# Expert results finished in slot order: gathered residual and branch rows, and a scatter straight into the output

## What is computed

```python
x = x + s * g                                   # block 0
xn = _layernorm(x, axis=-1)
s = _L1_attn_ref(xn, ...)                       # Y + X: the branch rows
# expert layer
route = jax.nn.sigmoid(x @ router_w)            # x is xn here
max_ind = jnp.argmax(route, axis=1)
max_prob = jnp.take_along_axis(route, max_ind[:, None], axis=1)
for e in range(num_experts):
    h = jax.nn.silu(x @ gate_w[e]) * (x @ up_w[e])
    out = out + jnp.where((max_ind == e)[:, None], h @ down_w[e], 0.0)
out = out * max_prob
# end of block 1
x = x + s * _silu(out)
```

## Time and profile before

| | us |
|---|---|
| median of 3 runs | 370.25 |
| lowest and highest run | 370.02, 370.71 |
| span of the profiled execution | 370.6 |

### The profile page before, as it was taken

The page is one execution under the profiler, slowest core; times in us unless marked ns, Lnnn a source line. Parts: engine busy times, 40 slices in busy tenths (PEclk is TensorE's granted clock), DMA queues, the critical chain, the costliest instruction groups (busy, mean ns, idle before and its releaser), DMA issues.

```text
span 370.6 us, 4637 instructions
## 1 busy us (share of the span) xinstructions
PE 326.3 (88%) x1598; PEld 191.5 (52%) x1598; DVE 239.2 (65%) x473; ACT 154.4 (42%) x279; POOL 62.8 (17%) x64
## 2 busy tenths in 40 slices
PE   3849859999999999999999999989968999999730
PEld 3426636545555454455554555556554576666420
DVE  3999895977666677877958510499793644433305
ACT  1614722476766655553664555203113322332300
POOL 4372480000011000000000000014570111211211
PEclk9958997999999999999999999996998999999965
DMA  7960000000000000000000050093029960111015
GB/s 262 405 161 0 2 0 3 0 3 1 0 4 0 3 0 3 0 0 3 2 2 1 0 171 2 2 371 138 31 92 329 435 240 30 30 42 44 17 44 200
DMA packets 9914, 28.46 MB, mean 77 GB/s; under 512 B 1342, under 2 KB 6559, under 8 KB 8608
## 3 DMA queue, kind: packets, MB, share of 16 engines
q1 hardware_dynamic: 8976, 26.01, 19.3%
q0 software_dynamic: 912, 2.12, 1.5%
HBM read 24.86 MB, written 5.55 MB: 82 GB/s over the span
## 4 chain that ended last, share of the span: by engine, by line
PE 72%; DVE 17%; DMA 4%; issue 2%; POOL 2%; ACT 1%; DVEq 0%; SPq 0%; POOLq 0%
PE ps L1532 11%; PE ps L1477 8%; PE ps L1445 8%; PE ps L1545 7%; PE ps L1467 7%; PE ps L1586 6%; PE ps L1600 6%; PE ps L1608 5%; PE ps L1382 3%; DVE xn L1014 3%; PE ps L1407 2%; DVE nmax L1069 2%; POOL slot_rows L779 2%; PE ps L1361 2%; PE ps L1576 1%
## 5 line engine op out<-in xcount | busy, mean ns | idle before, releaser
L1069 DVE TENSOR_REDUCE nmax<-ps 128x1 f32<-128x512 f32 x128 | 85.8, 688 | 34.4 <-PE ps L1445 33.7
L880 ACT ACTIVATE shared<-ps 128x512 f32<-128x512 f32 x128 | 74.2, 594 | 53.9 <-PE ps L1467 52.8
L1445 PE MATMUL ps<-experts 96*128 96x512 bf16 x128 | 48.2, 384 | 1.8 <-DVE experts L1076 1.2
L1467 PE MATMUL ps<-experts 99*128 99x512 bf16 x128 | 48.5, 382 | 0.0
L1545 PE MATMUL ps<-shared,experts 128*128 128x256 f32 x128 | 38.0, 386 | 0.0
L1477 PE MATMUL ps<-shared,experts 128*32 128x512 f32 x256 | 34.1, 605 | 0.3 <-ACT shared L880 0.3
L1445 PEld LDWEIGHTS ps<-experts 96*128 96x128 bf16 x128 | 12.5, 98 | 36.8 <-DVE nmax L1069 18.2
L1545 PEld LDWEIGHTS ps<-shared,experts 128*128 128x128 f32 x128 | 23.3, 191 | 9.7 <-issue 3.4
L1382 PE MATMUL ps<-late_weights,xnT 128*128 128x512 f32 (+1 forms) x64 | 25.0, 542 | 0.7 <-DVE shared L1035 0.7
L769 POOL TENSOR_TENSOR experts<-experts,late_weights 128x768 f32<-128x768 f32 x1 | 1.8, 1809 | 130.9 <-ACT experts L870 130.9
L888 ACT ACTIVATE experts<-ps 96x1024 bf16<-96x1024 bf16 x18 | 18.0, 1020 | 12.5 <-PE ps L1407 12.4
(11 more groups left out here) (204 smaller groups left out, 536.3 us busy)
## 6 DMA issues: line engine op xcount, KB each, us to landing
experts<-in_experts SPq DMA_DIRECT2D x8, 1536.0 KB, 10.6
shared<-in_wgu SPq DMA_DIRECT2D x1, 2048.0 KB, 11.1
slot_rows<-in_empty SPq DMA_DIRECT2D x1, 1950.0 KB, 19.6
late_weights<-slot_rows SPq DMA_DIRECT2D x9, 130.0 KB, 2.3
x<-in_x SPq DMA_DIRECT2D x2, 512.0 KB, 5.7
shared<-in_wdn SPq DMA_DIRECT2D x1, 1024.0 KB, 13.1
shared<-expert_results SPq DMA_DIRECT2D x4, 256.0 KB, 3.7
out_x<-x SPq DMA_DIRECT2D x4, 256.0 KB, 2.0
```

Source lines behind the costliest of these rows:

```text
L880: nc.scalar.activation(probs[:, n % 2, hh, :], ps[:, 2 + hh % 2, :], ACT.Exp, scale=float(HD) ** -0.5).then_inc(s["exp_done"], 1)
L1069: nc.vector.tensor_reduce(nmax[:, 4 * t + hh:4 * t + hh + 1], ps[:, m % 2, :], AX, ALU.max, negate=True).then_inc(s["max_done"], 1)
L1445: nc.tensor.matmul(ps[:, m % 2, :], qs[0:KS, b, GR * g + hh, P * t:P * t + P], ks[0:KS, b, g, :], start=True, stop=True).then_inc(s["score ...
L1467: nc.tensor.matmul(ps[:, 2 + hh % 2, :], ks[0:KM, b, g, P * t:P * t + P], qs[0:KM, b, GR * g + hh, :], start=True, stop=True).then_inc(s[" ...
```

## The change

Rows are finished in the order of the slots. Both operands of the end, x and the branch rows, go into one DRAM table of token rows (`token_rows`, 1024 rows of 2 KB: x, then s). For each tile POOL gathers its 128 rows of this table by token number into one of four buffers (`gathered`, which lies in the memory of `x`), three tiles ahead. DVE multiplies the result with the gathered branch row and adds the gathered x row; POOL scatters the finished rows by token number straight into the output. Token numbers are changed from p + 128 j to 8 p + j, so that the output's layout [128, 8, 256] is a plain table of rows.

SP stores x after it has issued the third expert's load, and the branch rows after the last branch step, ahead of all reloads of row slots. As the branch rows come late, the results of tiles 0 to 6 are kept in `held`, and `final` finishes them later: 0 and 1 after result 4 in tile 5, 2 and 3 in tile 6, 4 and 5 in tile 7, and 6 ahead of result 7 in tile 8. From tile 7 on `result` does it all. A row slot is now loaded again only when the finished rows of its tile have landed in the output. The reload of the results, the four products and additions at the end and the four output stores are gone. The end waits for the scatters and for the gathers of up to three tiles that aren't there (their rows are all out of bounds).

```diff
-    put("token", p[:, None] + P * np.arange(NT)[None, :])
+    put("token", p[:, None] * NT + np.arange(NT)[None, :])
...
+    xg_dram = nc.dram_tensor("token_rows", (TOK, 2 * D), F32, kind="Internal").ap()
+    xg_rows = xg_dram.rearrange("(p j) d -> p j d", p=P)
+    out_rows = out.rearrange("p j d -> (p j) d")
...
+        held = Sa[:, 0:D * HELD].rearrange("p (j n) -> p j n", j=HELD)
+        gathered = x[:].rearrange("p (a c) n -> p a (c n)", a=GATHERED)
...
                 if e == FIRST_EXPERTS - 1:
+                    sp.wait_ge(s["x1_part"], B * TB // 2)
+                    sp.dma_start(xg_rows[:, :, 0:D], x[:]).then_inc(s["x_stored"], 16)
...
+            sp.wait_ge(s["branch_ready"], NT // 2)
+            sp.dma_start(xg_rows[:, :, D:2 * D], gx[:]).then_inc(s["g_stored"], 16)
+
             def reload_rows(i):
                 if i + XR < MT:
                     sp.wait_ge(s["xs_T"], i + 1)
-                    sp.wait_ge(y_store[i % 2], 16 * (i // 2 + 1))
+                    sp.wait_ge(out_store[i % GATHERED], 16 * (i // GATHERED + 1))
                     load_rows(i + XR)
...
             sp.wait_ge(s["results_stored"], 1)
-            for q in range(NT // 2):
-                sp.dma_start(yg[:, 2 * q:2 * q + 2, :], y_dram.rearrange("(j p) d -> p j d", p=P)[:, 2 * q:2 * q + 2, :]).then_inc(result_sem[q], 16)
-            for q in range(NT // 2):
-                sp.wait_ge(s["out_ready"], q + 1)
-                sp.dma_start(out[:, 2 * q:2 * q + 2, :], x[:, 2 * q:2 * q + 2, :]).then_inc(out_sem[q], 16)
-            for q in range(NT // 2):
-                sp.wait_ge(out_sem[q], 16)
...
+            def gather(i):
+                if i >= GATHERED:
+                    pool.wait_ge(out_store[i % GATHERED], 16 * (i // GATHERED))
+                pool.wait_ge(x_sem[i % XR], 16 * (i // XR + 1))
+                nc.gpsimd.indirect_dma_start(
+                    out=gathered[:, i % GATHERED, :], out_offset=None, in_=xg_dram[:, :], in_offset=by_token(i),
+                    bounds_check=TOK - 1, oob_is_err=False).then_inc(gather_sem[i % GATHERED], 16)
+
             def store(i):
-                pool.wait_ge(s["y_ready"], i + 1)
+                pool.wait_ge(s["out_ready"], i + 1)
                 nc.gpsimd.indirect_dma_start(
-                    out=y_dram[:, :], out_offset=bass.IndirectOffsetOnAxis(ap=slot_row(i, TOKEN_COL, TOKEN_COL + 1).bitcast(I32), axis=0),
-                    in_=ysb[:, i % 2, :], in_offset=None, bounds_check=TOK - 1, oob_is_err=False).then_inc(y_store[i % 2], 16)
+                    out=out_rows[:, :], out_offset=by_token(i),
+                    in_=gathered[:, i % GATHERED, 0:D], in_offset=None, bounds_check=TOK - 1, oob_is_err=False
+                ).then_inc(out_store[i % GATHERED], 16)
+                if i + GATHERED - 1 < MT:
+                    gather(i + GATHERED - 1)
 
             def all_stored(n):
-                for a in range(2):
-                    pool.wait_ge(y_store[a], 16 * ((n + 1 - a) // 2))
+                for i in range(n, min(n + GATHERED - 1, MT)):
+                    pool.wait_ge(gather_sem[i % GATHERED], 16 * (i // GATHERED + 1))
+                for a in range(GATHERED):
+                    pool.wait_ge(out_store[a], 16 * ((n + GATHERED - 1 - a) // GATHERED))
                 pool.sem_inc(s["results_stored"], 1)
 
+            pool.wait_ge(s["x_stored"], 16)
+            pool.wait_ge(s["g_stored"], 16)
+            for i in range(GATHERED - 1):
+                gather(i)
             for i in range(SURE):
                 store(i)
...
             def result(k):
                 dve.wait_ge(s["e_down"], k + 1)
-                if k >= 2:
-                    dve.wait_ge(y_store[k % 2], 16 * (k // 2))
                 nc.vector.tensor_scalar_mul(ysb[:, k % 2, :], ps[:, 6, 0:D], slot_row(k, PROB_COL, PROB_COL + 1)).then_inc(s["y_half"], 1)
...
+                if k < HELD:
+                    dve.wait_ge(s["y_tanh"], k + 1)
+                    nc.vector.scalar_tensor_tensor(held[:, k, :], ytanh, 1.0, ysb[:, k % 2, :], ALU.add, ALU.mult).then_inc(s["y_ready"], 1)
+                    return
+                row = gathered[:, k % GATHERED, :]
+                dve.wait_ge(s["y_half"], k + 1)
+                dve.wait_ge(gather_sem[k % GATHERED], 16 * (k // GATHERED + 1))
+                nc.vector.tensor_tensor(row[:, D:2 * D], ysb[:, k % 2, :], row[:, D:2 * D], ALU.mult).then_inc(s["product_ready"], 1)
+                dve.wait_ge(s["product_ready"], k + 1)
                 dve.wait_ge(s["y_tanh"], k + 1)
-                nc.vector.scalar_tensor_tensor(ysb[:, k % 2, :], ytanh, 1.0, ysb[:, k % 2, :], ALU.add, ALU.mult).then_inc(s["y_ready"], 1)
+                nc.vector.scalar_tensor_tensor(row[:, D:2 * D], ytanh, 1.0, row[:, D:2 * D], ALU.add, ALU.mult).then_inc(s["y_ready"], 1)
+                dve.wait_ge(s["y_ready"], k + 1)
+                nc.vector.tensor_tensor(row[:, 0:D], row[:, D:2 * D], row[:, 0:D], ALU.add).then_inc(s["out_ready"], 1)
+
+            def final(k):
+                row = gathered[:, k % GATHERED, :]
+                dve.wait_ge(s["y_ready"], k + 1)
+                dve.wait_ge(gather_sem[k % GATHERED], 16 * (k // GATHERED + 1))
+                nc.vector.tensor_tensor(row[:, D:2 * D], held[:, k, :], row[:, D:2 * D], ALU.mult).then_inc(s["product_ready"], 1)
+                dve.wait_ge(s["product_ready"], k + 1)
+                nc.vector.tensor_tensor(row[:, 0:D], row[:, D:2 * D], row[:, 0:D], ALU.add).then_inc(s["out_ready"], 1)
+
+            finals = {SURE - 3: (0, 1), SURE - 2: (2, 3), SURE - 1: (4, 5), SURE: (6,)}
```

More of the change, by code:

```diff
@@ L47 @@
 VW = 32
+HELD = SURE - 1
+GATHERED = 4
 QK_AT = 8192 + 2048 + NI * S
@@ L799, in _ @@
             tiles_from(pool, n_tiles, SURE, store, all_stored)
-            for q in range(NT // 2 - 1, NT // 2):
-                pool.wait_ge(result_sem[q], 16)
-                pool.wait_ge(s["branch_ready"], NT // 2)
-                nc.gpsimd.tensor_tensor(ya[:, 2 * q:2 * q + 2, :], yg[:, 2 * q:2 * q + 2, :], gx[:, 2 * q:2 * q + 2, :], ALU.mult
-                                        ).then_inc(s["product_ready"], 1)
         @block.scalar
@@ L1283, in tile, with last_rows @@
                 nc.vector.tensor_tensor(hm[:, i % 2, :], gated[:, i % 2, :], ps[:, 2 + i % 2, :], ALU.mult).then_inc(s["e_h"], 1)
+                last_rows(i)
+            def last_rows(i):
+                if i >= SURE:
+                    for k in finals.get(i, ()):
+                        final(k)
                 if i:
                     result(i - 1)
+                if i < SURE:
+                    for k in finals.get(i, ()):
+                        final(k)
             for i in range(SURE):
@@ L1297, in _ @@
             n_tiles = dve.value_load(tiles_n[0:1, 0:1], min_val=SURE, max_val=MT)
[L1298 to L1316 removed]
+            tiles_from(dve, n_tiles, SURE, tile, last_rows)
         @block.tensor
```

35 lines of the change are left out of this document (10 added, 25 removed).

## The result

The changed kernel takes 364.45 us (median of four runs, 363.6 to 365.07) beside 370.42 us for the kernel before on the same chip: a ratio of 0.984, with an interval of 0.9805 to 0.9873. Five of those ten runs lie over 1.5% above the fastest and count as slow; the median of the other five is 365.12. The forecast was 361.2, in a range of 359.7 to 364.8: the first median lies just inside that range, the second above it. The sign and the path of the tail up to its last wait were right; the gain is 3.5 to 6 us where the forecast had 9.

The account below looks back on a forecast made before the run. PE bounds the expert tiles, then a 14.3 us tail leaves it idle. Scatter at 357.60, empty gather from 358.87 to 361.05, plus 0.5 to the end gives 361.55; less 0.35, 361.2 us, range 359.7 to 364.8.

Parts of the forecast that it names:

- To the start of the last scatter: Tail: scaling at 354.94, STT end at 356.34, residual addition to 356.83, GpSimd's scatter 0.77 us later at 357.60.
- Scatter to empty gather: Tail on GpSimd: consecutive indirect DMAs start 1.27 us apart, so the gather for absent tile 13 starts at 358.87.
- Empty gather to the end of the waits: Tail: the out-of-bounds gather lands after 2.18 us, at 361.05; bounds 0.96 to 2.4 us.
- Rival 1: Tail: the empty gather lands at once and the last scatter decides the end, 360.0 us; chance 0.12.
- From there to the end: Block end: 0.5 us from last landing to span end, with GpSimd's drain taken as 0 (bounds 0 and 3.4).
- rival 2: Block end: GpSimd's drain or code behind its nested branches is exposed, up to 3.4 us, giving 364.6; chance 0.21.
- the 0.35: Span to time: the runs' median, 370.25, lies 0.35 us below the profiled span of 370.6; taken off 361.55.
- reload of slot 8: Expert tiles: SP's reload takes 2.1 us to 327.2, PE transposes at 329.21; 2.0 us of cover, the tightest joint.
- Rival 3: Expert tiles: slot 8's reload is late and PE stalls about 5 us, total 366 to 368; chance 0.09.
- Rival 4: GpSimd's queue: 2 KB-row gathers cost far more to issue and bound the kernel, 378 at 3.3 us each; chance 0.05.
- Gather 7: Expert tiles: GpSimd's backlog lands this gather at about 338, 0.5 us after VectorE asks, inside VectorE's cover.
- VectorE beside GpSimd: Expert tiles: indirect-DMA issue doesn't hold VectorE, arithmetic does; otherwise up to 1.9 us a tile in tiles 5 to 7.

Follow-up runs that it names:

- second series: The changed kernel with no edit, measured again beside the kernel before with the experiments: 366.9 us (ten runs, 361.58 to 368.75), ratio 0.990.

## Why the prediction was right, and where it was not

**The tail, step by step.** Counted from the start of the last scaling (predicted at 354.94, found at 352.09):

- To the start of the last scatter: predicted 357.60 - 354.94 = 2.66, measured 354.83 - 352.09 = 2.74. The product did run beside the tanh (352.61 to 353.03) and cost nothing. A dependent 256-column step came 0.46 us after the one before, not 0.485, and GpSimd's start 0.83 us after its releaser, not 0.77.
- Scatter to empty gather: predicted 1.27, measured 1.33.
- Empty gather to the end of the waits: predicted 2.18 (between 0.96 and 2.4), measured 358.4 - 356.16 = 2.24. A gather with all its rows out of bounds costs what a full one of the same kind costs in the quickest case (2.1 us, view of L797 below). Rival 1, an end at the scatter's landing, is thereby out.
- From there to the end: predicted 0.5, measured 3.2. **This is the step that failed.** "POOL's last instruction has ended 1.2 us before the landing it waits for, so there is nothing left to drain" took the drain for a wait for running work. The kernel with the products on VectorE, the one with 14 more gathers and the early drains show a cost for every indirect DMA since the last drain, 82 ns each, due whenever the drain comes. Its bounds, 0 and 3.4, did hold it, and rival 2 with its 0.21 is what happened, and not the forecast with its 0.50: 361.2 + 2.8 = 364.0, against 364.45 in the first series. That the first median falls into the range is owed to rival 2's share of it.

Sum: 2.74 + 1.33 + 2.24 + 3.2 = 9.51, against 2.66 + 1.27 + 2.18 + 0.5 = 6.61 predicted.

**From span to time.** "The median of the runs lies 0.35 below that span" compared two executions, as did the sentence ahead of the prediction that took the profiled execution's span for its time. The time of one and the same execution was 1.8 us above its span in the kernel before, and the profiled execution was 2.2 us above the median span of 368.4. The two nearly cancel, so the 0.35 did little harm as a number, by luck, and was wrong as a relation. In the changed kernel the time outside the span is 2.45 us (2.10 to 2.57), 0.6 more. It is back at 1.83 to 1.87 without the empty gathers, or with SP waiting, or with the drain ahead of gather 7, but 2.26 with the three early drains and 2.4 where only result 7 is held. Why is open.

**The tiles.** Shifted by the 2.85 us that aren't the change's, the moved work came as forecast. The timelines of VectorE and GpSimd in the changed kernel around the first two finals (start us, us, line, operation, tiles, idle before and releaser; L1309 and L1311 are `final`):

```profile
318.07 0.42 DVE L1309 TENSOR_TENSOR x<-shared,x 128x256 f32<-128x256 f32 x1
318.53 0.42 DVE L1311 TENSOR_TENSOR x<-x 128x256 f32<-128x256 f32 x1
318.87 0.42 DVE L1309 TENSOR_TENSOR x<-shared,x 128x256 f32<-128x256 f32 x1
319.32 0.42 DVE L1311 TENSOR_TENSOR x<-x 128x256 f32<-128x256 f32 x1
319.67 0.68 DVE L1319 SCALAR_TENSOR_TENSOR gated<-tanh_g,ps 128x512 f32<-128x512 f32 x1
320.70 0.69 DVE L1323 TENSOR_TENSOR wl<-gated,ps 128x512 f32<-128x512 f32 x1 [0.36 <-PE ps L1640]
```

```profile
311.94 1.07 POOL L797 DMA_INDIRECT x<-token_rows,xs  x1 [37.22 <-DMA token_rows<-gx]
...
319.82 1.02 POOL L803 DMA_INDIRECT out_x<-x,xs  x1 [4.20 <-DVE x L1311]
```

Final 0 starts at 318.07 (predicted 320.95 - 2.85 = 318.10), and the pair takes 1.6 us up to the next tile's L1319, instead of 1.9. L1323 then waits for PE 0.36 us, so it isn't late at all. The first scatter starts at 319.82 (predicted 319.85). The branch store of 1 MB landed in 4.5 us (5.0 predicted), gather 0 started at 311.94 (312.35). The view of L803 in the changed kernel gives 2.2 to 4.5 us to landing; SP issued the reload of slot 8 at 322.36 (322.25 predicted); it took 2.8 us, where I had the 2.1 of the earlier trace rows, so it is in at 325.2, and PE transposes it at 326.42: 1.3 us of cover, 2.0 predicted. Rival 3 did not happen in this profile. (Its price took the 3.58 us of the last down products as what follows a pause of PE. In the kernel with the products on VectorE they took 2.00 us behind a like pause, 1.40 us instead of 1.32, so that doesn't always follow.)

The queue of GpSimd: an indirect DMA took 1.02 us instead of 0.96 as a rule (1.00 to 1.19), gather or scatter, with rows of 1 or 2 KB alike. Rival 4, that a gather costs far more to issue, is out: from 319.82 on GpSimd does 22 of them and still has idle stretches of 2.6 and 3.9 us.

**Gather 7** is the step inside the tiles that came out differently. Predicted was a wait of 0.5 us on VectorE; the timelines show the gather issued at 333.58 and VectorE waiting 2.72 us:

```profile
333.58 1.19 POOL L797 DMA_INDIRECT x<-token_rows,late_weights  x1 [1.14 <-DMA out_x<-x,late_weights]
```

```profile
337.44 0.43 DVE L1297 TENSOR_TENSOR x<-late_weights,x 128x256 f32<-128x256 f32 x1 [2.72 <-DMA x<-token_rows,late_weights]
```

Two sizes were off. The view of L797 gives the landing of a gather:

```profile
DMA to landing us min/median/max: 2.1/3.3/3.9
```

3.3 in the median, where I took the 2.4 of the earlier trace rows, which are stores of half the bytes. And gather 7 needs the buffer of store 3, whose landing GpSimd awaited for 1.14 us. The wait cost nothing: L1323 of that tile ran at 339.41 to 340.10 and PE wanted its result at 341.72.

The Trainium skill (DMA: Bandwidth & Descriptors, "Anatomy of one DMA") would have 2.0 us plus 256 KB over 436 GB/s, an estimate of 2.6 us for a full gather. The trace's quickest is below and its median above that, beside the row loads and scatters of the same tiles.

**VectorE beside GpSimd.** The forecast that GpSimd's issue work doesn't hold VectorE was right. L1297 reads two SBUF tensors of 256 columns; at 340.56 it took 0.42 us in the middle of the issue of L803 (340.39 to 341.41), and 0.42 us at 352.61, where GpSimd idled. The seven L1309, with two SBUF inputs as well, all took 418 to 426 ns. The Trainium skill (GPSIMD Engine Reference, "Key points") has VectorE instructions with two SBUF inputs contend with GpSimd for SBUF; for indirect DMAs this trace shows none of it.

**What stays open.** The median span of the changed kernel's second series is 2.4 us longer than the tail explains, and its times scatter (spans 359.0 to 366.2). Whether they scatter more than those of the kernel before isn't settled: that kernel had 367.8 to 370.8 on the same chip, but 365.7 to 371.3 and 365.8 to 370.9 on two others. In three of the ten profiles with the moved work (result 7 held; three early drains; one early drain) PE pauses 0.9 to 1.6 us ahead of a gate or down product in the tiles behind the fixed ones; in none of the four profiles of the kernel before and its variants. The same thing happens in all three. Here it is with one early drain (L963 copies the transposed rows that the gate product L1633 reads, L1290 is the scaling):

```profile
340.97 0.38 ACT L963 ACTIVATE xsT<-ps 128x256 f32<-128x256 f32 x1 [3.00 <-remote]
341.65 1.98 PE L1633 MATMUL ps<-experts,xsT 128*128 x4 [0.86 <-issue]
...
343.91 0.48 DVE L1290 TENSOR_SCALAR late_weights<-ps,xs 128x256 f32<-128x256 f32 x1 [3.21 <-remote]
```

PE's transposes had ended at 339.05, so ScalarE starts its copy 1.92 us late; in the changed kernel's profile it starts 0.04 us after them. VectorE starts the scaling 3.1 us after its down product has ended. So the tile is held up by ScalarE and VectorE, which stand still together although their operands are there; what lets them go on, the profile can't name. That the instructions of these nested tiles are fetched beside more transfers would fit, but no run tells it apart, and the queues that carry instructions moved as much, six packets and 0.07 MB from 320 to 356 us, in the kernel before as in these. Two smaller parts vary too. The pause ahead of the last tile's transposes is 1.02 to 1.54 us in ten of the fourteen profiles and 1.87 to 2.05 in four, all with the moved work. And the last down products take 2.00 us in some profiles of either kernel and 3.2 to 3.8 in others, where the granted clock is low (0.53 from 349 to 352 us in the changed kernel's profile, the 1.2 GHz level for most of it, and 1.00 in the kernel with the products on VectorE). So the gain that a median shows, 3.5 to 6 us, is the 6.2 us of the tail less something that comes and goes in the tiles, and less 0.6 outside the span.

## What to carry to other kernels

Trace a tail to the very last instruction of every engine: a drain that is hidden while GpSimd finishes early becomes part of the time the moment GpSimd is last, and it is as long as the number of indirect DMAs since the last drain says. Let another engine wait for GpSimd's last landing, issue no gather for a tile that isn't there, and pay for a drain where GpSimd idles; here these three took the tail from 9.51 to 5.41 us, 4.1 us beside the change's own gain of 3.5 to 6 in the median. And take the distance between span and time from one execution, and the place of the profiled execution among others from several spans, before the two are added.

## What the runs showed that I had not expected

- GpSimd's drain costs about 82 ns for each indirect DMA of 128 rows since the last one, and about 75 ns of its own: 0.21 us after 2, 1.13 after 13, 1.63 after 19, 2.60 after 30, 2.78 after 33, whether these moved rows of 1 KB, of 2 KB or nothing. It can be paid early.
- The drain also waits for GpSimd's transfers that are under way: it ended with the landing, 2.2 us after the start of the last scatter, where little else was due.
- A gather whose 128 rows are all out of bounds costs 1.02 us to issue, and lands 2.24 us after its start.
- Where a pause of PE has no releaser in its own chain, the timelines of the engines that feed it can have one: in all three such pauses ScalarE's copy came late.
